# Gate and experts in one program, and the mix's channel product on 64x64 blocks

## The reference, cut to what matters

```python
h = tok(x)                                   # 4 Fourier layers on 128 images of 64x64, 32 channels
h = concatenate([h, txt], axis=1)            # (128, 96, 64): 128 sequences of 96 tokens, 64 wide
h = h + attn(layernorm(h))
h = h + ffn(layernorm(h))

def fourier_layer_of_tok(v):                 # i of 4
    x1 = irfft2(mix of the low 12x12 modes of rfft2(v) by complex weights W1, W2)
    x2 = einsum('bcxy,cd->bdxy', v, w_w[i]) + w_b[i]
    v = batchnorm(x1 + x2)                   # relu after it in layers 0 to 2

def ffn(x):                                  # 8 experts, 256 hidden, top two, and a shared expert
    shared = gelu(x @ W1s + b1s) @ W2s + b2s
    rw = softmax(x @ Wr)
    topw, topi = top_k(rw, 2)
    topw = topw / sum(topw)
    mask = sum over the two of one_hot(topi, 8) * topw
    h = gelu(einsum('bsd,edf->bsef', x, W1p) + b1p)
    priv = einsum('bsef,efd->bsed', h, W2p) + b2p
    return shared + einsum('bsed,bse->bsd', priv, mask)
```

## Time and profile before

| | before |
|---|---|
| median of 3 runs | 2758.26 us (2756.05 to 2761.63) |
| the profiled execution, its own time | 2755.14 us |
| its span, first to last instruction | 2753.4 us |
| PE, DVE, ACT, POOL busy | 85%, 70%, 38%, 18% |
| mean granted TensorE clock | 0.932 of full speed |

### The profile page before, as it was taken

How to read it: one execution, slowest core, us unless ns; L and a number is a source line. 1 busy time by engine, 2 the same in 40 slices (tenths; PEclk the granted TensorE clock), 3 DMA queues, 4 the chain that set the end, 5 groups by cost and what they waited for, 6 DMA issues and landing times. The chain is left out here.

```text
span 2753.4 us, 191399 instructions
## 1 busy us (share of the span) xinstructions
PE 2334.1 (85%) x88271; PEld 1444.0 (52%) x88271; DVE 1924.8 (70%) x3293; ACT 1050.1 (38%) x1799; POOL 500.5 (18%) x619
## 2 busy tenths in 40 slices
PE   5799999977999997789999975876499826899998
PEld 3466666644666665456666642222277712444444
DVE  5688888865888886668888854004588863677776
ACT  3433333352333332523333333002136623677776
POOL 1034422200444221024442200000223200000000
PEclk9899999997999999989999997898789958999999
DMA  3266666615999996179999964896234203788886
GB/s 86 57 152 168 170 163 163 170 40 186 322 322 320 313 314 185 58 253 325 328 315 310 311 215 159 314 415 118 81 93 113 66 14 82 125 141 143 144 141 100
DMA packets 243410, 515.84 MB, mean 187 GB/s; under 512 B 65423, under 2 KB 114895, under 8 KB 222223
## 3 DMA queue, kind: packets, MB, share of 16 engines
q1 hardware_dynamic: 233736, 504.07, 64.4%
q10 hardware_dynamic: 9495, 9.34, 1.6%
HBM read 295.39 MB, written 214.78 MB: 185 GB/s over the span
## 5 line engine op out<-in xcount | busy, mean ns | idle before, releaser
L923 ACT ACTIVATE p_v<-p_ps,k_scale_bias 128x1024 f32<-128x1024 f32 x384 | 441.8, 1200 | 883.8 <-PE p_ps L794 883.8
L904 POOL COPY k_xm<-p_sp 64x288 f32<-64x288 f32 x372 | 260.2, 700 | 1181.0 <-DVE p_sp L327 1164.8
L317 DVE STREAM_TRANSPOSE p_vt<-p_v 128x1024 f32<-128x1024 f32 x384 | 451.2, 1213 | 6.4 <-ACT p_v L923 6.4
L794 PEld LDWEIGHTS p_ps<-k_idfty,p_t 32*64 32x64 f32 x24576 | 292.0, 135 | 178.5 <-issue 178.4
L2201 DVE TENSOR_TENSOR x_ht<-x_ht,x_mask 128x384 f32<-128x384 f32 x512 | 262.0, 554 | 149.7 <-ACT x_ht L2172 102.2
L2172 ACT ACTIVATE x_ht<-x_ph,w_b 128x384 f32<-128x384 f32 x576 | 303.4, 578 | 142.4 <-PE x_ph L2224 142.4
L322 DVE STREAM_TRANSPOSE p_at<-p_ps 128x1024 f32<-128x1024 f32 x192 | 228.5, 1228 | 149.6 <-PE p_ps L295 149.6
L794 PE MATMUL p_ps<-k_idfty,p_t 32*64 32x64 f32 x24576 | 319.8, 237 | 10.7 <-issue 10.7
L803 PEld LDWEIGHTS p_ps<-p_vt 128*32 128x32 f32 x24576 | 219.6, 109 | 99.8 <-issue 99.8
L2224 PE MATMUL x_ph<-x_et,w_w 64*64 64x384 f32 x2304 | 247.0, 494 | 12.7 <-DMA x_et<-expert_inputs 6.4
L2240 PE MATMUL x_pe<-x_ht,w_w 64*64 64x384 f32 x2304 | 245.0, 489 | 11.3 <-DVE x_ht L2201 10.2
(11 more groups left out here) (329 smaller groups left out, 2625.4 us busy)
## 6 DMA issues: line engine op xcount, KB each, us to landing
field<-p_v SPq DMA_DIRECT2D x768, 256.0 KB, 5.8
p_v<-field SPq DMA_DIRECT2D x128, 1024.0 KB
x_mask<-expert_weights SPq DMA_DIRECT2D x32, 1536.0 KB, 14.8
l_v<-field SPq DMA_DIRECT2D x16, 2048.0 KB, 25.8
k_xm<-field SPq DMA_DIRECT2D x12, 2048.0 KB, 28.7
at_cf<-state_coefficients SPq DMA_DIRECT2D x32, 384.0 KB
k_mixw<-field SPq DMA_DIRECT2D x4, 2048.0 KB, 26.1
k_mixw<-in_L_tok_fw_dram SPq DMA_DIRECT2D x48, 144.0 KB, 4.4
```

The source lines that it names most:

```text
L317: return nc.vector.transpose(cols(vt), cols(px.rearrange("p (g m) -> p g m", g=G)))
L794: ins = nc.tensor.matmul(ps[64 * a1:64 * a1 + 64, g, col:col + S], lines, K["idfty"][rows, :], start=False, stop=True, skip_group_check=True)
L904: nc.gpsimd.tensor_copy(view[64 * k:64 * k + 64, :, j, :, G * i:G * i + G], sp[64 * j:64 * j + 64, :, :, 16 * k:16 * k + M1].rearrange("p ...
L923: nc.scalar.activation(field[:, 2 * q:2 * q + 2, CH * half:CH * half + CH], ps[:, e, 2 * q:2 * q + 2, :], ACT.Relu, bias=bias, scale=scale ...
```

## The change

1. `gate_phase` and the `end_phase` behind it are gone. Its work stands at the head of `expert_phase`'s block, on the same engines.
2. The top two are picked on the logits and not on the softmax. The two weights are 1/(1+exp(l2-l1)) and exp(l2-l1)/(1+exp(l2-l1)), with an Exp over 96x128 elements. The ranks for ties are set on POOL.
3. `b2s` is added to the eight rows of `b2p` on POOL (the two weights of a token add up to one), and the block diagonal tile is made there by a multiplication with a 0/1 tile, in the place of a cleared tile with 16 loads into it. The addition over all of `h2` is gone.
4. The eight transposes of the gates are made into PSUM in one row, copied by two DVE copies of 128x384, and stored by two DMAs. PE then runs 16 bias matmuls over four PSUM banks, and DVE adds them to `h2`.
5. This stands between experts 1 and 2 of iteration 0. The inputs of iteration 0 are loaded before it, and `hidden` of experts 0 and 1 runs before it. PE, and DVE too, go on only when all 16 bias rows are added.
6. The gates lie in DRAM by sequence, expert, token. A mask load reads one run of 12 KB for each partition. The mask tile is sequence, expert, token, so that an expert's slice is four runs of 96 elements.
7. The mix's channel product multiplies two image groups at a time: 4 matmuls of 64 rows and 64 columns per unit, with the zeros between the two blocks.

```diff
@@ mix_tensor
         for j in range(2):
-            for r in range(2):
-                for k in range(2):
-                    rows = slice(64 * k + C * r, 64 * k + C * r + C)
-                    at = 64 * j + C * r
-                    ins = nc.tensor.matmul(zb[at:at + C, nb, k, :], zw[rows, rows], unit(K, n, j)[rows], start=True, stop=True)
+            for k in range(2):
+                rows, at = slice(64 * k, 64 * k + 64), slice(64 * j, 64 * j + 64)
+                ins = nc.tensor.matmul(zb[at, nb, k, :], zw[rows, rows], unit(K, n, j)[rows], start=True, stop=True)
@@ expert_phase, sync
+            for b in range(16):
+                eng.dma_start(b2r[E * b:E * b + E, :], d["b2p"]).then_inc(s.bias_in, 16)
+            eng.dma_start(b2s[:, :], d["b2s"] ... broadcast_to([P, D])).then_inc(s.bias_in, 16)
...
+                if isinstance(i, int) and i == 0:
+                    for half in range(2):
+                        eng.wait_ge(s.gate_out, half + 1)
+                        rows = gates.rearrange("(t b) e x -> (b e) t x", b=16)[:, GB // 2 * half:GB // 2 * half + GB // 2]
+                        eng.dma_start(rows, mt[:, GB // 2 * half:GB // 2 * half + GB // 2, :]).then_inc(s.gate_stored, 16)
+                    eng.wait_ge(s.gate_stored, 32)
                 at_least(eng, s.t_ready, 2 * E * (i - 1))
-                eng.dma_start(mask[:, par], gates.rearrange("(o e) (n b) t -> n o e (b t)", o=1, b=NB)[i]
-                              .broadcast_to([P, E, CT])).then_inc(m_in[par], 16)
+                eng.dma_start(mask[:, par].rearrange("p b e t -> p (b e t)"), gates.rearrange("(n o b) e t -> n o (b e t)", o=1, b=NB)[i]
+                              .broadcast_to([P, NB * E * T])).then_inc(m_in[par], 16)
@@ expert_phase, vector
+            def one_of(pick, values, best):
+                c.then(ve.tensor_tensor(pick, values, per_token(best), ALU.is_equal))
+                c.then(ve.tensor_tensor(pick, pick, ranks, ALU.mult))
+                c.then(ve.tensor_reduce(m[:, 2, :], pick, AX.X, ALU.max))
+                c.then(ve.tensor_tensor(pick, ranks, per_token(2), ALU.is_equal))
+            def top_two():
+                ve.tensor_reduce(member, eye as (b e), AX.X, ALU.add).then_inc(s.block_ready, 1)
+                c.then(ve.tensor_reduce(m[:, 0, :], gate[:, :, :], AX.X, ALU.max))
+                dve.wait_ge(s.rank_ready, E)
+                one_of(first, gate, 0)
+                c.then(ve.scalar_tensor_tensor(out=rest, in0=first, scalar=-3.0e38, in1=gate, op0=ALU.mult, op1=ALU.add))
+                c.then(ve.tensor_reduce(m[:, 1, :], rest[:, :, :], AX.X, ALU.max))
+                c.then(ve.tensor_tensor(m[:, 3, :], m[:, 1, :], m[:, 0, :], ALU.subtract))
+                dve.sem_inc(s.rest_ready, 1)
+                one_of(second, rest, 1)
+                dve.wait_ge(s.rest_exp, 1)
+                c.then(ve.tensor_scalar(m[:, 5, :], m[:, 4, :], 1.0, None, ALU.add))
+                c.then(ve.reciprocal(m[:, 6, :], m[:, 5, :]))
+                c.then(ve.tensor_tensor(m[:, 7, :], m[:, 4, :], m[:, 6, :], ALU.mult))
+                c.then(ve.tensor_tensor(first, first, per_token(6), ALU.mult))
+                c.then(ve.tensor_tensor(second, second, per_token(7), ALU.mult))
+                ve.tensor_tensor(gate, first, second, ALU.add).then_inc(s.gate_ready, 1)
+                for half in range(2):
+                    dve.wait_ge(s.gate_turned, half + 1)
+                    ve.tensor_copy(half of mt, ps_e[:, 1, half, 0:CT]).then_inc(s.gate_out, 1)
+                for k in range(2 * GB):
+                    dve.wait_ge(s.bias_done, k + 1)
+                    rows = h2[:, 8 * k:8 * k + 8, :]
+                    ve.tensor_tensor(rows, rows, ps_e[0:T, k // 2 % 2, k % 2, :] ..., ALU.add).then_inc(s.bias_added, 1)
+                dve.wait_ge(s.bias_added, 2 * GB)
...
-                    ve.tensor_tensor(h, h, mask[:, par, j // 2 - 1, :], ALU.mult).then_inc(s.t_ready, 1)
+                    h = h.rearrange("p (b t) -> p b t", b=NB)
+                    ve.tensor_tensor(h, h, mask[:, par, :, j // 2 - 1, :], ALU.mult).then_inc(s.t_ready, 1)
@@ expert_phase, gpsimd
+            for e in range(E):
+                gp.memset(rank[:, e:e + 1], float(E - e)).then_inc(s.rank_ready, 1)
+            pool.wait_ge(s.bias_in, 16 * 17)
+            gp.tensor_tensor(b2r[:, :], b2r[:, :], b2s[:, :], ALU.add).then_inc(s.bias_ready, 1)
...
+            gp.tensor_tensor(b2, b2r broadcast over 16, member spread over 64, ALU.mult).then_inc(s.bias_ready, 1)
@@ expert_phase, tensor
+            def gates_turned():
+                pe.wait_ge(s.gate_ready, 1)
+                for t in range(GB):          # GB = 8
+                    ins = nc.tensor.transpose(ps_e[:, 1, 2 * t // GB, ...], gate[:, 16 * t:16 * t + 16, :] ..., eye)
+                    if t % (GB // 2) == GB // 2 - 1:
+                        ins.then_inc(s.gate_turned, 1)
+            def biases():
+                pe.wait_ge(s.gate_out, 2)
+                pe.wait_ge(s.bias_ready, 2)
+                for k in range(2 * GB):
+                    at_least(pe, s.bias_added, k - 3)
+                    nc.tensor.matmul(ps_e[0:T, k // 2 % 2, k % 2, :], mt[:, k // 2, :], b2 half ...).then_inc(s.bias_done, 1)
+                pe.wait_ge(s.bias_added, 2 * GB)
...
                 for e in range(E + 1):
+                    if not later and e == 2:
+                        gates_turned()
+                        biases()
                     hidden(i, par, r, e)
```

More of the change, by code:

```diff
@@ L2108, in expert_phase @@
-def expert_phase(nc, sems, W, X, out, e2t_dram, gates):
+def expert_phase(nc, sems, W, X, d, out, e2t_dram, gates):
     s = sems
@@ L2136, in expert_phase @@
         o_out, e_in, m_in = [s.u_out0, s.u_out1], [s.u_in0, s.u_in1], [s.y_in0, s.y_in1]
+        GB = B // 16
+        gate, h2 = W["gate"], W["h2"]
+        first, second, rest = (sb(x, [T, B, E]) for x in ("first", "second", "rest"))
+        m, rank = sb("m", [T, 8, B]), sb("rank", [T, E])
+        b2r, b2s, b2, member = sb("b2r", [P, D]), sb("b2s", [P, D]), sb("b2", [P, 16, D]), sb("member", [P, 16])
+        mt = sb("mt", [P, GB, T])
+        ranks = rank[:, :].rearrange("p (o e) -> p o e", o=1).broadcast_to([T, B, E])
         block = ctx.enter_context(nc.Block())
@@ L2165, in _ @@
         def _(act):
+            act.wait_ge(s.rest_ready, 1)
+            nc.scalar.activation(m[:, 4, :], m[:, 3, :], ACT.Exp).then_inc(s.rest_exp, 1)
             def body(i, par, r, last):
@@ L2179, in _, with per_token @@
             ve = nc.vector
+            c = Chain(dve, s.step)
+            def per_token(j):
+                return m[:, j, :].rearrange("p (n o) -> p n o", o=1).broadcast_to([T, B, E])
+            def one_of(pick, values, best):
+                c.then(ve.tensor_tensor(pick[:, :, :], values[:, :, :], per_token(best), ALU.is_equal))
+                c.then(ve.tensor_tensor(pick[:, :, :], pick[:, :, :], ranks, ALU.mult))
+                c.then(ve.tensor_reduce(m[:, 2, :], pick[:, :, :], AX.X, ALU.max))
+                c.then(ve.tensor_tensor(pick[:, :, :], ranks, per_token(2), ALU.is_equal))
@@ new lines, in top_two @@
+            def top_two():
+                ve.tensor_reduce(member[:, :], W["eye"][:, :].rearrange("p (b e) -> p b e", e=E), AX.X, ALU.add).then_inc(s.block_ready, 1)
+                c.then(ve.tensor_reduce(m[:, 0, :], gate[:, :, :], AX.X, ALU.max))
+                dve.wait_ge(s.rank_ready, E)
+                one_of(first, gate, 0)
+                c.then(ve.scalar_tensor_tensor(out=rest[:, :, :], in0=first[:, :, :], scalar=-3.0e38, in1=gate[:, :, :],
+                                               op0=ALU.mult, op1=ALU.add))
+                c.then(ve.tensor_reduce(m[:, 1, :], rest[:, :, :], AX.X, ALU.max))
[6 more added lines that the diff above has]
+                c.then(ve.tensor_tensor(m[:, 7, :], m[:, 4, :], m[:, 6, :], ALU.mult))
+                c.then(ve.tensor_tensor(first[:, :, :], first[:, :, :], per_token(6), ALU.mult))
+                c.then(ve.tensor_tensor(second[:, :, :], second[:, :, :], per_token(7), ALU.mult))
+                ve.tensor_tensor(gate[:, :, :], first[:, :, :], second[:, :, :], ALU.add).then_inc(s.gate_ready, 1)
+                for half in range(2):
+                    dve.wait_ge(s.gate_turned, half + 1)
+                    ve.tensor_copy(mt[:, GB // 2 * half:GB // 2 * half + GB // 2, :].rearrange("p t x -> p (t x)"), ps_e[:, 1, half, 0:CT])\
+                        .then_inc(s.gate_out, 1)
+                for k in range(2 * GB):
+                    dve.wait_ge(s.bias_done, k + 1)
+                    rows = h2[:, 8 * k:8 * k + 8, :]
+                    ve.tensor_tensor(rows, rows, ps_e[0:T, k // 2 % 2, k % 2, :].rearrange("p (b d) -> p b d", b=8), ALU.add).then_inc(s.bias_added, 1)
+                dve.wait_ge(s.bias_added, 2 * GB)
@@ L2294, in tokens @@
         end_phase(nc, sems)
-    gate_phase(nc, sems, W, d, gates)
```

(3 more changed lines are left out.)

128 lines of the change are left out of this document (28 added, 100 removed).

## The result

The changed kernel takes 2668.05 us, the median of 4 runs (2662.97 to 2675.13), against 2757.95 us before (2756.05 to 2761.63, 4 runs). The ratio is 0.9673, with a 95% interval of 0.9655 to 0.9692.

What follows compares the result with a forecast made beforehand. DVE's chain bounds the gate's pick, PE the experts' loop. Gains of 49.1 us at the head, 3 at the loop's entry and 1.5 in the channel product sum to 53.6, giving 2704 us, range 2690 to 2714.

Steps and rivals of the forecast that it cites:

- The mechanism of the merge and its sizes: From the gates to `outputs` of expert 1: shorter pick, faster stores and mask, dense bias rows; 46.1 us gained there.
- GpSimd's hindrance: Gate pick: POOL and DVE may hinder each other, between nothing and POOL's whole time; taken as nothing.
- the 3.0 behind it: Experts after `outputs` of expert 1: next five groups take 3.2 us with the clock up, for 6.2 cold.
- a slower head: Bias rows and stores: low clock, stops for code or slow 384 B stores lose 5 to 12 us; chance 0.15.
- a slower mask: Mask load: 128 partitions reading the same 12 KB land slower, about 2780 us at 20 us landing; chance 0.02.
- The loop does not get shorter: that rival: Experts' loop: a fast mask frees the 0.47 us wait at each `turn`, 14 us in all, giving 2690; chance 0.06.
- 0.01 per unit, 0.7 us, and 0.8 for fewer instructions to fetch: Mix's channel product: the 64x64 form gains 1.5 us in all, bounds a loss of 2 and a gain of 11.5.
- The rival that 64x64 blocks pay: Mix's channel product: cheaper mode changes take up to 0.16 us off each unit, giving 2694; chance 0.12.
- 16 more cost 0.08: Channel product: 32 records hold PE 1.09 us against 1.01 for 16, so the number of records is not the cost.
- a third of it goes: 3 us, bounds 0 and 9: Experts' loop entry: of 9 us in PE's code stops and cold stretches, a shorter mask flight removes a third.

Runs made afterwards that it cites:

- The kernel with quarters: Kernel before with the channel product on 64x64 blocks, each matmul cut into four of 128 columns (192 records a unit): 2817.62 us, ratio 1.0237.
- the one with the fewest records: Changed kernel with the mode mix also on 64x64 blocks, 80 records a unit for 144, weights read with a wrong stride: 2659.49 us, ratio 0.9664.

## Why the prediction was wrong

**The mechanism of the merge and its sizes: right.** Gates ready after 21.3 us (19.8 forecast; the 1.6 are GpSimd's hindrance, which I had named and set at nothing). Each store landed 2.3 us after its issue, for 4. The mask took 6.5 us in the loop, for 7.0 and not the 14.8 of the old runs (at the head two masks were issued 1.6 us apart and the second took 10.8, but nothing waited for either). The Trainium skill (DMA: Bandwidth & Descriptors, Specifications) has full rate from 512 B on, which does not describe this load: its runs of 1.5 KB and of 12 KB are both above that and took 14.8 us against 6.5. Bias rows in 16.8 us to the next group, for 18.3, since the clock rose 4 us after their start (granted 0.50 until 2224.2, then 1.00) and not 6.2; the transposes ahead of them had begun at 2218.02. The sum to `outputs` of expert 1 was forecast as 46.1 and is 47.7 (42.4 us from the phase's start for 43.1, and a barrier ahead of it shorter by 0.9), and the 3.0 behind it is 3.0. The rivals of a slower head and of a slower mask did not come about. The loop does not get shorter: that rival is refuted by the unchanged 13.14 and its 0.48.

**First failed step: "0.01 per unit, 0.7 us, and 0.8 for fewer instructions to fetch".** The first number was right: the hold went from 1.01 to 1.02. The rival that 64x64 blocks pay is refuted too; the same blocks cut in two pay nothing (0.9995). What failed is the 0.8. The test that "16 more cost 0.08" was read from the image loop, whose code is repeated, and used for the mix, whose code is written out and runs once a layer. There, 160 records a unit arrive at 65 to 67 a us and the work needs 73. The rows in front of me had it: `592.14` to `593.15` was taken for a unit's price, while the trace had 2.76 us from one unit to the next on average and 2.2 of work in them. The term was 23 us by the product alone (16 to 29), about half of it in the mixes. The other half lies behind them, in the first passes of the image loops: in the 80 us after each of the first three mixes TensorE has "issue" stops of 34 to 37 us in sum in the four kernels with 160 records a unit, and of 24 to 33 in the other nine. That it pays there for fetching which fell behind in the mix is my reading and not shown. The kernel with quarters fits it (time to spare in the mix, 28 us of stops), the one with the fewest records does not (33 us), though its "between" is as low as with 144. So for this half the runs show that it comes and goes with the 16 records, and not how.

**Second failed step: "a third of it goes: 3 us, bounds 0 and 9".** The stops at the loop's ends went altogether, 11.4 us of turns. The cause was right (code waited for while the DMA engines carry the mask), the scaling wrong: a third, because "a mask in flight half as long" was treated as a delay in proportion. In the kernels with short runs a packet of code began 0.4 to 3.6 us into each of the long stops; with long runs, at a share of 0.42, there is no such stop at all. And I counted the entry alone; the exit, 1.4 us here and up to 9.2 in the experiments, had the same stop.

**What was luck.** Of the 92.2 us between the two profiled executions some 5 belong to neither edit: about 4 ahead of the gates and 1.5 behind the last `turn`. The parts named above make 85 to 87: 47.7 and 3.0 at the head, 11.4 in the loop, and 23 to 25 by the product.

## What to carry to other kernels

Price an edit to straight-line matmul code by records per us over a whole unit, beside the array's time: if the pitch from unit to unit is longer than the work in it and TensorE shows "issue" stops, removing instructions pays though no matmul gets faster, until the next engine bounds. A DMA that is hidden can still cost, by its packets, the engine that fetches code at that moment; look at the DMA share, not at GB/s. And when a single edit hits something that bounds everything upstream, compare the whole span, stage by stage, before reading only the part that the diff names.

## What the runs showed of the hardware

- In the mixes, straight-line matmul code reached TensorE at 65 to 67 records a us, in packets of 16 KB that started 3.9 us apart (117 in 2753 us). The mode mix by itself ran at 110 records a us.
- 1.5 MB to all partitions: 14.8 us in runs of 1.5 KB at a share of 0.85, 6.5 us in runs of 12 KB at 0.42, for the same 140 GB/s in the loop.
- The channel product on 64x64 blocks held TensorE for 1.02 us as 4 matmuls of 512 elements, 1.04 as 8 of 256, and 2.50 as 16 of 128.
- A packet of code began inside each of nine stops of TensorE at the ends of the experts' loop, in the kernels whose mask comes in runs of 1.5 KB; with 12 KB runs there was no such stop.
- A VectorE operation of 1.22 us took 2.81 beside GpSimd's product, and that one 2.78 for 1.90.
